# Indirect transfers without a bound on their indices, in a two-layer graph network kernel

## The reference

```python
h = max(layernorm(x), 0)
msg = relu(h[src] + edge_attr)                 # one row per edge
agg = zeros_like(h).at[dst].add(msg)           # summed by target
z = (h + agg) @ W1 + b1                        # 256 -> 512
z = batchnorm over all nodes, gamma, beta; relu; @ W2 + b2    # 512 -> 256
z = graph layernorm (one graph), then graph norm by channel, relu
x = x + h + z
h = max(layernorm(x), 0)
agg = segment_sum((h @ M)[src], dst)
out = x + relu(h @ W + agg)
```

## Time and profile before

| | |
|---|---|
| median of 3 runs | 2876.51 us |
| profiled execution, span | 2469.0 us |
| profiled execution, time outside of the span | not recorded |
| PE busy | 2368.3 us (96%) |
| DVE busy | 2053.6 us (83%) |
| ACT busy | 1713.4 us (69%) |
| POOL busy | 1712.1 us (69%) |
| POOL transfers, line 430, 433, 439 (99 each) | 1051, 1013, 1068 ns |
| POOL transfers, line 1011 and 1458 (392 each) | 1181, 980 ns |
| POOL transfers, line 1781 and 1789 | 1033, 1010 ns |

### The profile page before, as it was taken

How to read it: one execution, slowest core, us unless ns; L and a number is a source line. 1 busy time by engine, 2 the same in 40 slices (tenths; PEclk the granted TensorE clock), 3 DMA queues, 4 the chain that set the end, 5 groups by cost and what they waited for, 6 DMA issues and landing times. The chain is left out here.

```text
span 2469.0 us, 49485 instructions
## 1 busy us (share of the span) xinstructions
PE 2368.3 (96%) x12271; PEld 2015.0 (82%) x12271; DVE 2053.6 (83%) x5707; ACT 1713.4 (69%) x3449; POOL 1712.1 (69%) x1599
## 2 busy tenths in 40 slices
PE   7999998799999999999999999979998989989997
PEld 5888886588888888888888888859887989969976
DVE  7999997598888888888888888957776767759986
ACT  6999997366666666666666666548887878846654
POOL 5777776677677666677667767527776767747776
PEclk8999998899999999999999999989999999999999
DMA  7999995313444444444444444369999999645653
GB/s 252 281 278 275 277 279 162 120 58 126 162 156 155 147 146 164 154 145 145 163 153 144 144 161 153 127 232 411 411 411 400 401 391 396 260 155 162 172 169 115
DMA packets 255790, 531.59 MB, mean 215 GB/s; under 512 B 55280, under 2 KB 142601, under 8 KB 255650
## 3 DMA queue, kind: packets, MB, share of 16 engines
q1 hardware_dynamic: 195250, 459.36, 51.0%
q0 software_dynamic: 59808, 70.24, 10.3%
q10 hardware_dynamic: 592, 0.54, 0.1%
HBM read 340.23 MB, written 286.84 MB: 254 GB/s over the span
## 5 line engine op out<-in xcount | busy, mean ns | idle before, releaser
L1011 POOL DMA_INDIRECT ar<-sum_table,idx x392 | 462.9, 1181 | 177.6 <-issue 96.5
L1058 ACT ACTIVATE r<-pair,bnC,bnA 128x512 f32<-128x512 f32 x392 | 305.9, 781 | 380.7 <-PE pair L1259 378.2
L1458 POOL DMA_INDIRECT x1d_table<-x1r,slot x392 | 384.0, 980 | 152.3 <-issue 115.0
L1166 DVE CAST rH<-r 128x512 fp32r<-128x512 f32 x392 | 386.1, 985 | 96.6 <-ACT r L1058 96.6
L1684 PE MATMUL pair<-Ws,h1T 128*128 128x256 f32 x1568 | 359.3, 382 | 6.8 <-DVE orr L1592 5.3
L1684 PEld LDWEIGHTS pair<-Ws,h1T 128*128 128x128 f32 x1568 | 291.8, 191 | 48.4 <-issue 11.4
L1275 PE MATMUL bank<-rH,W2h 128*128 128x512 f32 (+1 forms) x784 | 305.4, 390 | 1.8 <-ACT yr L1072 1.8
L1275 PE MATMUL bank<-rL,W2h 128*128 128x512 f32 (+1 forms) x784 | 305.3, 389 | 0.0
L1275 PE MATMUL bank<-rH,W2l 128*128 128x512 f32 (+1 forms) x784 | 304.6, 389 | 0.0
L1175 DVE TENSOR_TENSOR rL<-r,rH 128x512 fp32r<-128x512 f32 x392 | 276.6, 706 | 13.5
L826 PE MATMUL bank<-hr 128*128 128x257 f32 (+1 forms) x1568 | 274.7, 329 | 10.1 <-ACT hr L525 10.1
(11 more groups left out here) (246 smaller groups left out, 5243.9 us busy)
## 6 DMA issues: line engine op xcount, KB each, us to landing
xr<-in_x SPq DMA_DIRECT2D x186, 512.0 KB, 3.8
x_table<-x1r SPq DMA_DIRECT2D x97, 512.0 KB, 15.2
out<-orr SPq DMA_DIRECT2D x97, 512.0 KB
xh_table<-xr SPq DMA_DIRECT2D x89, 512.0 KB, 2.6
yT_table<-yr SPq DMA_DIRECT2D x89, 512.0 KB
xh_kept<-xh_table SPq DMA_DIRECT2D x57, 512.0 KB
y_stays<-yT_table SPq DMA_DIRECT2D x57, 512.0 KB, 15.9
xhr<-xh_table SPq DMA_DIRECT2D x32, 512.0 KB, 15.4
```

The source lines that it names most:

```text
L1011: pool.indirect_dma_start(ar[0:p, s, j, :], None, sum_table[:, :], bass.IndirectOffsetOnAxis(ap=idx[0:p, s, j:j + 1], axis=0), bounds_chec ...
L1058: act.activation(r32[:, m, 0:n], z_ps[m][:, 0:n], ACT.Relu, bias=bnC[:, m:m + 1], scale=bnA[:, m:m + 1]).then_inc(r_kept, 1)
L1166: dve.tensor_copy(rH[:, s, m, 0:n], r32[:, m, 0:n]).then_inc(rh_kept, 1)
L1458: pool.indirect_dma_start(x1d_table[:, :], bass.IndirectOffsetOnAxis(ap=slot[0:p, part, s * T + j:s * T + j + 1], axis=0), x1r[0:p, s, j, ...
```

## The change

The gathers of stage 1 (`e_s`, `e_d`), the early gathers at the end of stage 3, the gathers of stage 4 and the id scatter of stage 1 lose their bound. The scatter to `x1d_table`, the gathers from `sum_table`, the scatter to `out` and the branch for unsorted edges keep it. So that every index is valid, the target column is held to the last node, and `spot` sends each unused lane to a row of its own behind the part of `id_table` that is read: the table grows by 99 x 128 words, and DVE works `spot` out with two operations more.

```diff
-    id_table = nc.dram_tensor("id_table", (P * COLS, 1), I32, kind="Internal").ap()
+    id_table = nc.dram_tensor("id_table", (P * COLS + ET * P, 1), I32, kind="Internal").ap()
...
                     pool.indirect_dma_start(e_s[:, s, :], None, x[:, :],
-                                            bass.IndirectOffsetOnAxis(ap=index[:, t, 0:1], axis=0),
-                                            bounds_check=NODES - 1, oob_is_err=False).then_inc(sd_in[s], 16)
+                                            bass.IndirectOffsetOnAxis(ap=index[:, t, 0:1], axis=0)
+                                            ).then_inc(sd_in[s], 16)
...
                     pool.indirect_dma_start(id_table[:, :],
                                             bass.IndirectOffsetOnAxis(ap=spot[:, t:t + 1], axis=0),
-                                            index[:, t, 3:4], None,
-                                            bounds_check=P * COLS - 1, oob_is_err=False).then_inc(id_out[s], 16)
+                                            index[:, t, 3:4], None).then_inc(id_out[s], 16)
...
-                dve.tensor_copy(index[:, :, 1], dst_f[:])
+                dve.tensor_scalar(index[:, :, 1], dst_f[:], float(NODES - 1), None, ALU.min)
...
-                node = index[:, :, 2]
+                node = index[:, :, 1]
...
-                dve.tensor_scalar(parts[:, 3, :], node, 16, 16, ALU.logical_shift_right,
-                                  ALU.logical_shift_left).then_inc(spot_parts, 1)
+                dve.tensor_scalar(parts[:, 3, :], index[:, :, 3], float(P * COLS), None,
+                                  ALU.add).then_inc(spot_parts, 1)
...
-                dve.tensor_tensor(parts[:, 2, :], parts[:, 2, :], parts[:, 3, :], ALU.add).then_inc(spot_parts, 1)
+                dve.tensor_tensor(parts[:, 2, :], parts[:, 2, :], parts[:, 3, :], ALU.subtract).then_inc(spot_parts, 1)
                 dve.wait_ge(spot_parts, 2)
-                dve.tensor_tensor(spot[:], parts[:, 0, :], parts[:, 2, :], ALU.add).then_inc(spots_made, 1)
+                dve.tensor_tensor(parts[:, 0, :], parts[:, 0, :], parts[:, 2, :], ALU.add).then_inc(spot_parts, 1)
+                dve.wait_ge(spot_parts, 3)
+                dve.tensor_tensor(parts[:, 0, :], parts[:, 0, :], once_last[:], ALU.mult).then_inc(spot_parts, 1)
+                dve.wait_ge(spot_parts, 4)
+                dve.tensor_tensor(spot[:], parts[:, 0, :], parts[:, 3, :], ALU.add).then_inc(spots_made, 1)
```

More of the change, by code:

```diff
@@ L384, in _ @@
                                  table[full + shift:EDGES].rearrange("(a p) -> a p", a=1)).then_inc(idx_loaded, 16)
-                sp.dma_start(id_table.rearrange("(p t) a -> p (t a)", t=COLS), no_rows[:]).then_inc(ids_clear, 16)
+                sp.dma_start(id_table[0:P * COLS, :].rearrange("(p t) a -> p (t a)", t=COLS),
+                             no_rows[:]).then_inc(ids_clear, 16)
                 for k in range(1, 4):
@@ L413, in _ @@
                 sp.wait_ge(ids_set, 1)
-                sp.dma_start(ids[:, 0:COLS], id_table.rearrange("(p t) a -> p (t a)", t=COLS)).then_inc(ids_in, 16)
+                sp.dma_start(ids[:, 0:COLS], id_table[0:P * COLS, :].rearrange("(p t) a -> p (t a)", t=COLS)
+                             ).then_inc(ids_in, 16)
                 sp.wait_ge(ids_in, 16)
@@ L430, in edge @@
                     pool.indirect_dma_start(e_s[:, s, :], None, x[:, :],
-                                            bass.IndirectOffsetOnAxis(ap=index[:, t, 0:1], axis=0),
-                                            bounds_check=NODES - 1, oob_is_err=False).then_inc(sd_in[s], 16)
+                                            bass.IndirectOffsetOnAxis(ap=index[:, t, 0:1], axis=0)
+                                            ).then_inc(sd_in[s], 16)
                     pool.indirect_dma_start(e_d[:, s, :], None, x[:, :],
-                                            bass.IndirectOffsetOnAxis(ap=index[:, t, 1:2], axis=0),
-                                            bounds_check=NODES - 1, oob_is_err=False).then_inc(sd_in[s], 16)
+                                            bass.IndirectOffsetOnAxis(ap=index[:, t, 1:2], axis=0)
+                                            ).then_inc(sd_in[s], 16)
                     if t == 0:
@@ L1469, in _ @@
                     pool.indirect_dma_start(early_rows(t), None, x1_table[:, :],
-                                            bass.IndirectOffsetOnAxis(ap=index[:, t, 0:1], axis=0),
-                                            bounds_check=NODES - 1, oob_is_err=False).then_inc(early_in, 16)
+                                            bass.IndirectOffsetOnAxis(ap=index[:, t, 0:1], axis=0)
+                                            ).then_inc(early_in, 16)
                 pool.wait_ge(early_in, 16 * EARLY)
@@ L1781, in gather @@
                     pool.indirect_dma_start(source_rows(s), None, x1_table[:, :],
-                                            bass.IndirectOffsetOnAxis(ap=index[:, t, 0:1], axis=0),
-                                            bounds_check=NODES - 1, oob_is_err=False).then_inc(s4_in[s], 16)
+                                            bass.IndirectOffsetOnAxis(ap=index[:, t, 0:1], axis=0)
+                                            ).then_inc(s4_in[s], 16)
                 def scatter(t):
```

## The result

The changed kernel takes 2884.2 us, median of ten runs (2873.0 to 2892.2), beside 2873.8 of ten runs of the kernel before in the same comparison: ratio 1.0031, 95% interval 1.0016 to 1.0046. Slower by some 9 us, where 6 less had been forecast. A second comparison of the changed kernel gave 1.0034 [1.0015, 1.0054], so it is not chance, although it is small: the kernel before compared with itself came out at 0.9983 [0.9966, 0.9999].

What follows compares the result with a forecast made beforehand. Stage 1's steady part was taken as paced by full engines, its tail and stage 4 after the first third by GpSimd. Terms -3.4 - 3.6 + 0.1 + 0.5 = -6.4 us gave 2876.5 to 2870, range 2855 to 2886.

Steps and rivals of the forecast that it cites:

- The sum's own time: Whole kernel: differences of the profiled span, 2469.0 us, carried one for one to the median of the runs, 2876.51 us.
- x: How much shorter an indirect transfer with its 0.30 us gets without its bound: taken as 0.04 us.
- Rival B: Stages 1 and 4: the bound is dear, 0.12 us a transfer; 2861 us, at its ceiling 2857; chance 0.29.
- A: The bound is free, within 0.01 us a transfer, or savings go back in waits for DVE; 2876 us; chance 0.17.
- C: Slower, mainly stage 1: transfers without a bound take 0.05 us longer; 2895 us; chance 0.14.
- part 2: Stage 1: the id scatter writes every lane, 2,480 words more; 0.1 us over the tail of 10 tiles.
- Stage 4, -3.4 us: Stage 4: 85 gathers in GpSimd's back-to-back row, each 0.04 us shorter, take 3.4 us off the end.
- Stage 1, -3.6 us: Stage 1's tail: keeps GpSimd's 2.4 us in hand and gains 0.12 us for each of 10 tiles.
- rival C's lever: Stage 1: GpSimd has no spare time, so from tile 6 every lengthening adds to tile 98's start: 13.8 us.
- Parts 2 and 3, +0.6 us: Stage 1: extra words written by the id scatter, +0.1 us, and two more DVE index operations, +0.5 us.
- The rule on the ports: Stage 1: DVE and GpSimd lock shared SBUF ports, which would bring the sum nearer 0 than 7 us.

Runs made afterwards that it cites:

- the odd profile: The kernel before, unchanged, as profiled before the prediction: span 2469.0 us, where the median of its runs was 2876.51; it did not return in later profiles.
- e0: The kernel before, unedited, run and profiled again against itself: ratio 0.9983, profiled span 2873.0 us.
- e2: Kernel before with only the id scatter unbounded, with its longer table and index arithmetic; all gathers keep their bound: ratio 1.0007.
- e3: Kernel before with the id scatter's longer table and arithmetic, its bound moved to the table's end so no lane is rejected: ratio 1.0013.
- e7: Kernel before plus a 128 x 256 memset on GpSimd behind each output scatter of stage 4: ratio 0.998.
- e6: Kernel before plus a 128 x 256 memset on GpSimd behind each id scatter of stage 1: ratio 0.9986.
- e5: Kernel before with only the id table lengthened by 12,672 rows that nothing writes or reads: ratio 1.0003.
- e12: Kernel before with stage 4's output step on VectorE leaving out its SBUF tensor, the added target rows: ratio 1.0006.
- e9: Kernel before plus a 128 x 256 GpSimd memset behind each id scatter of stage 1 and each output scatter of stage 4: ratio 0.9927.
- e10: Kernel before plus a 128 x 512 GpSimd memset behind each id scatter of stage 1 and each output scatter of stage 4: ratio 0.9837.
- e13: Kernel before plus a 128 x 512 GpSimd memset behind each of the 392 scatters of stage 3: ratio 0.9772.
- e14: Kernel before plus 128 x 512 GpSimd memsets behind the transfers of stages 1, 3 and 4: ratio 0.964, 2746.3 us.
- e16: Kernel before plus four 128 x 512 memsets in a row behind each tile's fourth scatter in stage 3: ratio 1.0109.
- e17: Kernel before plus twelve nops on GpSimd behind each scatter of stage 3: ratio 0.9996, scatters still 1.28 us apart.

## Why the prediction was wrong

**The sum's own time: the step that failed.** The prediction saw that the profiled span was 407.5 us short of the runs, wrote that no row shows what lies around the span, and carried differences over one for one. What lies around it is 1.7 us. The rest lay inside: comparing the odd profile with e0, which is 404.0 us longer, stage 1 is some 133 us longer, stage 3 some 200 and stage 4 some 68, while stage 2 has its length. Every pace was read off an execution that the timed runs don't resemble.

**x.** Right in size: 0.05 us for a gather and 0.03 for the id scatter, forecast 0.04, and the 0.30 us untouched. That the scatter's bound alone saves nothing (e2 against e3) the prediction did not foresee; it had reasoned from rejected lanes of two scatters. Rival B (0.12) is refuted by these rows, and so is A's first half (within 0.01). A's second half, that what is saved goes back into waits for DVE, is what stage 4 shows. C had the sign of the result, but by transfers that get longer, and they got shorter. In part 2 a difference is miscounted: 12,672 - 10,200 is 2,472, which changes nothing.

**Stage 4, -3.4 us.** Zero: from first to last output scatter the two profiles of the changed kernel take 311.5 and 311.3 us, e0 311.0. It rested on GpSimd going back to back from the first scatter on the earlier trace rows. Ordinarily it waits 56 us for DVE in 290, DVE's stops set the period of 10 us in both kernels, and 0.33 us more per pair doesn't slow it (e7).

**Stage 1, -3.6 us and rival C's lever.** Neither is there. "There POOL has no spare time at all" held in the earlier trace rows; ordinarily it waits 128 to 149 us for ACT, and 0.33 us more per tile costs nothing (e6). No gain of the tail can be made out either: the last id scatter starts at 550.0 and 555.8 us in the two profiles of the changed kernel, at 556.5 in e0 and at 550.6 in e5.

**Parts 2 and 3, +0.6 us.** The scatter with all its side work, with or without its bound, stays within 0.13% (e2, e3); a size of 0.6 us can't be seen.

**The rule on the ports.** The prediction weighed the Trainium skill's rule that DVE and GpSimd lock each other out of a shared pair of SBUF ports (SBUF — State Buffer, "Who interferes with whom"), by which a shorter transfer would partly be spent waiting for the lock. The transfers kept what they gained: the shortest, the median and the mean of the id scatter all fell (989, 990 and 1001 ns against 1012, 1018 and 1030). The same section says that a DVE instruction with two SBUF inputs contends with a GpSimd instruction that reads SBUF. The step that stops reads only one tensor from SBUF, so it is not that case, and with none from SBUF it stopped as before (e12). What holds DVE is not shown.

**Why slower and not merely the same.** No case of the prediction had a loss with shorter transfers, and its cause stays open. Shown: a memset behind one of GpSimd's three transfers of a tile in stage 1, behind one of two in stage 4 and behind each scatter in stage 3 makes the kernel faster (e9, e10, e13, e14), in e10 the stops of stage 4 are gone with it, and the change costs more beside such memsets: 0.3% as it is, 0.7% beside e9, 1.0% beside e10 (the last two can't be told apart by their intervals), in those profiles mostly in stage 1. The reading that fits is that transfers which follow each other closely stop VectorE, and that the change brings them 0.03 to 0.05 us closer. It is not shown. Whether the distance counts, the rate over a tile or the memset's write was not separated (e16, e17), no run puts 0.05 us back behind each changed transfer, the change's other parts (the extra words, the longer arithmetic) were not tried beside a memset, and in single profiles 9 us over 2870 aren't located. Closeness alone is not enough either: in the odd execution GpSimd's transfers stood closest of all, back to back at 2.65 us a pair, and VectorE's longest wait there, from 2216 to 2443 us, was 1.1 us. What differed in that execution is open too.

## What to carry to other kernels

Before any sum, set the profiled span and its own run time beside the median of the runs. If they are 14% apart, paces and slack in that profile are no basis, and the rest of the argument needs another execution. Test a claimed bottleneck by adding a known small cost to it: 0.33 us more on a "full" engine that costs nothing refutes the claim in one run. When an added cost makes a kernel faster, look at the spacing of what that engine issues as well as at its load. And before a control decides between two theories, add up what it asks of its engine: if that alone is more than the stage's pace, as in e16, it can't show the gain that it tests for.

## What the runs showed of the hardware that was not expected

- A bound on an indirect gather of 128 rows of 1 KB costs 0.05 us of 1.03. Taken from a scatter of single words alone it saves nothing (median 1.017 against 1.018 us, e2 and e3); with the gathers ahead of it unbounded as well the scatter takes 0.990.
- Rows of GpSimd's indirect transfers 1.28 us apart go, in all but the odd execution, with stops of 3 to 9 us on VectorE, during which the other compute engines run dry; with a memset between them, at 1.69 us apart, stage 3 took 65 us less and the kernel ran 2.3% faster.
- A memset on GpSimd between transfers is cheap in distance: 0.54 us of work adds 0.41 us start to start, since the gap shrinks from 0.30 to 0.17. Four in a row behind the fourth transfer add all of their 2.48 us (e16).
- The mean granted clock was 0.93 to 0.94 of full speed in ordinary executions of both kernels, 0.957 in e14, 0.98 in the odd one. It isn't what stops VectorE: through four stops of e0, from 2655 to 2695 us, it was granted 2.4 GHz all the time.
